# Where attention's first rows are loaded, on whose queue, and when GpSimd's weight split starts

## The reference

```python
B, S, D, H = (4, 256, 256, 16)     # here b = 1, s = 1024
DK = D // H                        # 16
Q, K, V = (proj(Wq, bq), proj(Wk, bk), proj(Wv, bv))     # heads of 16 columns
scores = jnp.einsum('bhqd,bhkd->bhqk', Q, K) / scale     # scale = sqrt(DK)
scores = jnp.where(causal[None, None], -jnp.inf, scores)
attn = jax.nn.softmax(scores, axis=-1)
ctx = jnp.einsum('bhqk,bhkd->bhqd', attn, V)
out = jnp.einsum('bsd,ed->bse', ctx, Wo) + bo
```

## Time and profile before

| | us |
|---|---|
| median of 3 runs (range) | 1139.42 (1137.17 to 1140.31) |
| the profiled execution, its own time | 1135.98 |
| its span from the first to the last instruction | 1134.4 |

### The profile page before, as it was taken

How to read it: one execution, slowest core, us unless ns; L and a number is a source line. 1 busy time by engine, 2 the same in 40 slices (tenths; PEclk the granted TensorE clock), 3 DMA queues, 4 the chain that set the end, 5 groups by cost and what they waited for, 6 DMA issues and landing times.

```text
span 1134.4 us, 18322 instructions
## 1 busy us (share of the span) xinstructions
PE 864.2 (76%) x6048; PEld 506.0 (45%) x6049; DVE 552.8 (49%) x1051; ACT 387.5 (34%) x627; POOL 490.1 (43%) x538
## 2 busy tenths in 40 slices
PE   3199917277978847994689999758688855899995
PEld 1056603122222223662457777523334433577774
DVE  5623345467686352335513333458489755233334
ACT  3322202044455412221145555226402121555551
POOL 2228848888810021212234443123588731444431
PEclk9999957588798967996579999859899975899997
DMA  8224335655510010102843333230000044434323
GB/s 299 68 61 121 114 99 183 207 169 179 174 37 13 2 38 24 34 19 71 323 133 120 130 119 107 93 125 1 0 1 0 1 193 172 142 116 134 116 88 126
DMA packets 45580, 117.72 MB, mean 104 GB/s; under 512 B 10273, under 2 KB 23346, under 8 KB 44626
## 3 DMA queue, kind: packets, MB, share of 16 engines
q0 software_dynamic: 19280, 69.09, 19.1%
q1 hardware_dynamic: 21634, 43.64, 10.8%
q10 hardware_dynamic: 4608, 4.20, 1.1%
HBM read 90.16 MB, written 26.74 MB: 103 GB/s over the span
## 4 chain that ended last, share of the span: by engine, by line
PE 62%; DVE 15%; DMA 8%; POOL 5%; ACT 5%; issue 4%; SPq 1%; ACTq 0%; DVEq 0%; POOLq 0%
PE psum L490 18%; PE psum L518 13%; PE psum L1178 6%; PE psum L502 5%; PE psum L1638 4%; DVE mem L1272 2%; PE psum L174 2%; DMA mem<-w2l_dram 2%; PE psum L1153 2%; POOL mem L222 2%; DVE XTl L143 1%; PE psum L473 1%; PE psum L1665 1%; DMA max_dram<-mem 1%; ACT XTh L164 1%
## 5 line engine op out<-in xcount | busy, mean ns | idle before, releaser
L490 PE MATMUL psum<-mem 128*128 x984 | 233.3, 392 | 6.0 <-ACT psum L587 5.6
L518 PE MATMUL psum<-mem 128*128 x1536 | 178.2, 273 | 4.7 <-DVE mem L730 4.7
L518 PEld LDWEIGHTS psum<-mem 128*128 128x128 f16 x1536 | 149.9, 98 | 23.2 <-issue 5.6
L490 PEld LDWEIGHTS psum<-mem 128*128 128x128 f16 x984 | 98.8, 100 | 116.4 <-issue 20.4
L800 POOL DMA_INDIRECT y_dram<-mem x64 | 63.8, 997 | 164.5 <-DVE mem L738 161.7
L795 POOL DMA_INDIRECT mem<-xn_dram,mem x64 | 64.8, 1013 | 127.0 <-PE psum L473 109.5
L1230 ACT ACTIVATE mem<-psum 128x512 f32<-128x512 f32 (+1 forms) x160 | 80.0, 552 | 110.7 <-PE psum L1161 66.6
L1272 DVE TENSOR_REDUCE mem<-psum 128x2 f32<-128x1024 f32 (+2 forms) x96 | 89.1, 951 | 58.4 <-PE psum L1131 36.4
L730 DVE TENSOR_TENSOR mem<-psum,mem 128x512 f16<-128x512 f32 x128 | 82.4, 686 | 56.1 <-ACT mem L599 56.1
L719 DVE TENSOR_TENSOR mem<-psum,mem 128x256 f16<-128x256 f32 x64 | 27.1, 423 | 160.8 <-ACT mem L581 160.8
L174 PE MATMUL psum<-ident,mem 128*128 128x128 f32 x96 | 32.5, 441 | 95.3 <-DVE mem L148 95.3
(11 more groups left out here) (242 smaller groups left out, 1403.5 us busy)
## 6 DMA issues: line engine op xcount, KB each, us to landing
stage<-in_w POOLq DMA_DIRECT2D x20, 480.0 KB, 4.7
stage<-in_w POOLq DMA_DIRECT2D x16, 512.0 KB, 3.9
w2h_dram<-mem POOLq DMA_DIRECT2D x20, 240.0 KB, 2.9
w2l_dram<-mem POOLq DMA_DIRECT2D x20, 240.0 KB, 3.9
xn_dram<-mem ACTq DMA_DIRECT2D x32, 128.0 KB, 6.5
mem<-w2h_dram SPq DMA_DIRECT2D x2, 2048.0 KB, 13.3
mem<-w2l_dram SPq DMA_DIRECT2D x2, 2048.0 KB, 17.9
mem<-y_dram SPq DMA_DIRECT2D x16, 256.0 KB, 5.2
```

The costliest lines, as they stand in the source:

```text
L490: ins = eng.matmul(out, a[:, p, k, :], w[:, at], start=(gated and i == 0), stop=(i == 3 * KD - 1), skip_group_check=not gated)
L518: ins = eng.matmul(c.bank(6)[:, 0:D], a[:, q * half + j, :], w[:, at], start=(i == 0), stop=(i == 3 * CF - 1))
```

## The change

SyncE waits for the six stores of e = 0 alone, loads the rows of pair 0, and only then issues the six stores of e = 1. Those it waits for before the first `max_rows`. The rows of pairs 1 and 2 are issued by ScalarE, after its last bias and rounding of Q and K, when the stores of e = 0 have landed. The later `stacks` stay with SyncE. GpSimd's first load of w2 also waits for the first scores (`s_st(1)`).

```diff
-    s_pd = n("pd", 16 * 12)
+    s_pd = [n(f"pd{e}", 16 * 6) for e in range(KD)]
...
+    def stacks(eng, p):
+
+        slot = p % STACKS
+        for m, dst in (("wq", qs), ("wk", ks)):
+            for j in range(2):
+                rows = A[m + "_dram"][:, (2 * p + j) * DK:(2 * p + j + 1) * DK, :]
+                eng.dma_start(dst[64 * j:64 * j + QK_ROWS, slot, :], rows).then_inc(s_ld[slot].sem, 16)
...
                 for g, part_ in enumerate(ORDER[m]):
-                    eng.dma_start(A[m + "_dram"][g, e * P:(e + 1) * P, :], qk[m][part_][:, e, :]).then_inc(s_pd.sem, 16)
-        eng.wait_ge(*s_pd(16 * 12))
-        eng.wait_ge(*s_m(1))
-        for p in range(STACKS):
-            stacks(p)
+                    eng.dma_start(A[m + "_dram"][g, e * P:(e + 1) * P, :], qk[m][part_][:, e, :]).then_inc(s_pd[e].sem, 16)
+            if e == 0:
+                eng.wait_ge(*s_pd[0](16 * 6))
+                eng.wait_ge(*s_m(1))
+                stacks(eng, 0)
+        eng.wait_ge(*s_pd[1](16 * 6))
         for p in range(PAIRS):
             for s in range(2):
                 max_rows(p, s)
             if p and p + STACKS - 1 < PAIRS:
                 eng.wait_ge(*s_st(2 * NS * p))
-                stacks(p + STACKS - 1)
+                stacks(eng, p + STACKS - 1)
...
     def act(eng):
...
+        eng.wait_ge(*s_pd[0](16 * 6))
+        eng.wait_ge(*s_m(1))
+        for p in range(1, STACKS):
+            stacks(eng, p)
         for p in range(PAIRS):
             for i in range(NS):
...
         eng.wait_ge(*stage_free)
+        eng.wait_ge(*s_st(1))
```

More of the change, by code:

```diff
@@ L1045, in sync @@
         eng.dma_start(maskf[:, :, :], A["causal"].rearrange("p (a b) -> p a b", a=4)).then_inc(s_c.sem, 16)
[L1047 to L1053, removed]
         def max_rows(p, s):
```

## The result

| | before | changed |
|---|---|---|
| median, us | 1139.87 (12 runs) | 1126.6 (12 runs) |
| ratio of the changed kernel's time to before's | | 0.9881, 95% from 0.9856 to 0.9906 |
| profiled execution's span, us | 1134.4 | 1121.1 |

The forecast was 1125 in a range of 1117.5 to 1132.5; the changed kernel is 1.2% faster (0.9 to 1.4%). The changed kernel's L1046 is before's L1053, L1071 is L1070, L1059 and L1064 are L1058 and L1063, L1127 and L1133 are L1125 and L1131, L1155 is L1153, L1180 is L1178, L1278 is L1272, L1297 is L1291.

The account below looks back on a forecast made before the run. The attention layer was taken as a chain of waits, its start bound by row loads on three DMA engines and the store of maxima. First scores -15.8 plus GpSimd's +1.3 gave -14.5 us: median forecast 1125, range 1117.5 to 1132.5.

Parts of the forecast that it names:

- Stores of e = 0: Start of the attention layer: the last of these stores lands at 193.2 us (192.5 to 194.5), without GpSimd's loads beside it.
- Loads of pair 0: SyncE's four early loads land at about 203.5, so pair 0's maxima start then and not at 212.97: 9.5 us.
- Equal shares of the queues: On the three DMA engines, SyncE's and ScalarE's full queues each get half the rate of 25 kB/us.
- C: Rival, 15%: pair 0 served almost alone, landing at 200.5 to 201.5, e = 1 by 208; gain 18 to 21, 1120.
- A: Rival, 12%: three engines serve the stores last; e = 1 lands at 214.7, first scores 219.9; gain 12.4, 1128.
- B: Rival, 10%: ScalarE's loads crowd out pair 0's, landing up to 210.8; first scores 221.5 to 222; gain 10.5, 1130.
- The new wait: SyncE holds the first store of maxima, turned by 207.5, until e = 1 lands at about 211.3: some 3.8 us.
- The way back of the maxima: From the first store of maxima, landing at about 213.9, through two loads to first scores at 216.5, 15.8 us earlier.
- The page against the second queue: Trainium skill's objection: issuing from several engines saves sequencer time only, since all run on the same DMA engines.
- GpSimd beside more pairs: GpSimd's split runs beside some 2.3 more pairs, slowing normalise casts: +1.3 us, bounds -5.3 to +5.3, further +2.5 for the clock.
- D: Rival, 12%: GpSimd beside pairs 3 to 5 is dear; both casts hit, clock falls again, +5.3 + 2.5; 1131.5.
- E: Rival, 4%: slower; each pair GpSimd newly accompanies costs 5.3 us, 12 us in all, against B's 10.5 gain; 1141.

Follow-up runs that it names:

- gp_wait_only: Kernel before plus one line: GpSimd's first load of w2 waits for the first scores; ratio 0.9927 to before.
- act_after_first: Changed kernel with ScalarE's eight loads held until pair 0's rows have landed; ratio 0.9828 to before, 0.9846 when run again.
- one_queue: Changed kernel with pairs 1 and 2 loaded by SyncE behind the stores of e = 1, not by ScalarE; ratio 0.9874 to before.
- rows16: Changed kernel with each head's 48 rows read in the order row, part (16 x 3 x 1024, not 3 x 16 x 1024); ratio 0.9868 to before.
- gp_early: Changed kernel without GpSimd's wait for the first scores, so its w2 split starts as early as before; ratio 1.0007 to before.
- rows16_gp_later: Changed kernel with 16 x 3 x 1024 loads, ScalarE's held until pair 0's rows landed, GpSimd's first load until the fourth score piece; ratio 0.9818 to before.
- after_again: The changed kernel run once more, unaltered, on the same chip as three other runs; ratio 0.9901 to before.

## Why the prediction was right, step by step

*Stores of e = 0*: 193.2 forecast, 192.96 measured. Right.

*Loads of pair 0*: 203.5 forecast for PE's start, 205.00 measured. The term was 1.7 us short, 10.3 us from the first issue in place of 12.0. By my bound four loads alone took 7.1 us (193.2 to 200.3); they take 8.2 (gp_wait_only, 199.22 to 207.4) to 8.9 us (act_after_first). The start is what I had wrong: I let the engines run at 25 kB/us from 193.8 and so counted 50 kB each by 195.8. In the three microseconds from 193 the whole machine moved 16, 16 and 31 kB, 21 kB for each of three engines, and only in the fourth 68.

*Equal shares of the queues*: e = 1 landed at 212.9 (211.3 forecast), neither by 208 as in C nor at 214.7 as in A. By this time alone A is as near as the forecast, and the first scores at 218.51 lie nearer A's 219.9 than my 216.5. What rules A out is that some 176 kB were still to move once e = 1 had landed, and that the new wait is 3.9 us and not 7. From pair 0's landing to that of e = 1 it took 8.0 us, and 98 kB at half of 25 kB/us are 7.8: the equal shares fit. B and C are out by PE's start at 205.00, for which they had about 210 and 200.5. That ScalarE's loads were what slowed e = 1 is shown by act_after_first, 6.8 us in place of 13.4.

*The new wait*: 3.8 us forecast, 3.9 measured, in its place.

*The way back of the maxima*: 5.2 us forecast from issue to scores, 5.6 measured. First scores 216.5 forecast, 218.51 measured, a gain of 13.8 and not 15.8: the term was 2 us too large, by the two above.

*The page against the second queue*: by the Trainium skill (DMA: Bandwidth & Descriptors, Issuing engines are not separate DMA queues) it saves issue time only. one_queue agrees for the sum, 0.4 us; for one small DMA the queue did matter, 10.0 us behind the loads in its own queue and 3.0 beside them. With the same page's rule on the number of engines (section Why a DMA increments its semaphore by 16 and not by 1) rows16 agrees: with a slowest dimension of 16 in place of 3, the share from 196 to 204 us rises from 0.62 to 0.88, and no loads are left where the changed kernel runs on at 0.20. What I had not concluded from my own count of three engines was the order of sizes: I wrote the gain down as one of the early loads, and it is in the main one of GpSimd's wait. By the four corners (before, gp_wait_only, gp_early, changed), that line alone wins 11.5 us to the first scores, the loads alone 0, both 14.4.

*GpSimd beside more pairs*: +1.3 forecast, -2.4 in one trace of the changed kernel and +2.0 in the other. D (+7.8) and E (+12) are out by both. The pairs that GpSimd newly accompanies took 18.5 to 19.9 us in the first trace; in the second one of them took 22.7. Which instruction of DVE is slow beside GpSimd changes too: in the first trace the subtraction behind the cast at pair 1 (2.46 us for L1311, 0.69 otherwise) and nothing at pair 3, in the second the product and the cast at pair 3 (1.93 us for L1302, 1.37 for L1309, 0.43 each otherwise). I had counted two casts beside GpSimd; its split ended at 348.7, so that in the first trace pair 5's normalise was hit as well (2.37 and 1.37 us). The scatter of the term, 4.4 us between two executions of one program, is in part the clock's and in part this.

*What I missed.* GpSimd's start at the first scores moves its stream against the rounds of maxima of pairs 1 and 2. Stores of 8 KB took 4.62 and 9.41 us where they had taken 1.4 and 7.1, and PE waited 1.46 and 1.72 us for rows, which before happened nowhere in these pairs. It is 3.2 us within the 24.03 us stretch; that GpSimd's new place is the cause is my reading, no run tests it alone. And 3.3 us went at L899, far from the change. It came in both traced executions of the changed kernel and in neither of act_after_first, which suggests that it goes with the program, but four traces don't show it: of all 14 traces six have it, and a seventh a short one. What brings it stays open; by its size it would take back a quarter of this gain (3.3 of 13.3 us).

*The sum*: -14.5 us forecast, -13.3 measured between the two spans and as much between the medians. In the trace it comes of 13.8 at the first scores (15.8 forecast), another 2.4 in the loop (a loss of 1.3 forecast) and 2.9 lost behind the layer, for which I had no term. The mechanism held, but that the sum came out within 1.2 us is partly luck, since the errors cancel. The second traced execution of the same program, equal up to the first scores, was 11.9 us ahead at the layer's end and 3.3 us at the program's.

## What to carry to other kernels

When a DMA's share of the engines is a small constant, count the engines before moving the DMA: here one reordered view in the kernel before took 13.6 us off the way to the first scores, nearly the 14.4 of order, queue and timing together (in time 8.7 against 13.6 us, with overlapping intervals). Undo the parts of such a change one by one, since the part that looks like a side condition (GpSimd begins later) can be most of the effect. And when a wait is taken away, look at what clock the next stretch is granted before counting the time as won: in rows16 the pair behind it ran at 0.78 and took 4 us longer, though the pair after that was faster again.

## What the runs showed of the hardware

- Loads whose DRAM view is 3 x 16 x 1024 moved 73 to 76 GB/s at a share of 0.20 to 0.21 once the other engines had nothing to move. From 196 to 204 us, with the stores of e = 1 beside them, the engines moved 233 GB/s at 0.62; as 16 x 3 x 1024 the same loads and stores moved 279 GB/s at 0.88 in that stretch.
- A store of 8 KB lands in 1.4 us in a quiet queue, in 3.0 to 4.8 us when another queue fills the same engines, and in 10.0 to 12.6 us right behind eight loads of its own queue (in the 12.6 GpSimd streamed beside them).
- PE's granted clock fell to 0.50 at about 205 in the changed kernel, after PE had been busy for 0.4 of the 4 us from 200, and between 204 and 208 in rows16, in which it was busy for 1.7 of 4 us. It stayed there through pair 0's maxima and was back at 1.00 from about 222 in the changed kernel, from 238 in the kernel before, and from 223.5 in rows16, though its scores began 6 us sooner than in the changed kernel. That goes with 2.8 of the 4 us that rows16's first pair took longer. In rows16_gp_later it was back from 219.7 and the first pair took 24.0 us, but the next three ran at 0.84 to 0.85 and the loop was no shorter: that an earlier return gives time back at the end was not shown.
- Many of the pairs of 160 matmuls fall on steps: 18.3 to 18.7 us at a granted 1.00, 19.7 to 20.0 at 0.91, 20.7 to 21.1 at 0.83 to 0.84. Others are longer than their clock says, as 21.06 us at 1.00 in rows16, in which DVE's cast and subtraction took 2.02 and 2.38 us, and 22.71 at 0.85 in after_again.
